# Four fused sequence layers on one core: the state matrices turned by VectorE and by way of memory, and the gate product in two passes over x

## The reference, cut to what matters

```python
x = x + y * mask                      # y: each head convolved with its kernel K[h], up to 1024 taps
x = x + x @ W1.T + 2 * sum_e gate[e] * (x @ A[e].T) @ B[e].T   # gate: softmax of the two best of 8 logits x @ Wr.T
x = x + x @ W2.T + 0.5 * (x @ lora_A[label]) @ lora_B.T        # label: one of 5, by batch row
x = x + x @ w_eff.T                   # w_eff: quantized weight plus a low-rank part
```

## Time and profile before

| | us |
|---|---|
| median of three runs | 1013.91 |
| lowest and highest of them | 1013.37, 1016.0 |
| the profiled execution | 1015.38 |
| its span, first to last instruction | 1013.5 |
| granted TensorE clock, mean over the span | 0.998 |

### The profile page before, as it was taken

The page is one execution under the profiler, slowest core; times in us unless marked ns, Lnnn a source line. Parts: engine busy times, 40 slices in busy tenths (PEclk is TensorE's granted clock), DMA queues, the critical chain, the costliest instruction groups (busy, mean ns, idle before and its releaser), DMA issues.

```text
span 1013.5 us, 16370 instructions
## 1 busy us (share of the span) xinstructions
PE 994.4 (98%) x4767; PEld 799.7 (79%) x4767; DVE 823.2 (81%) x1617; ACT 454.1 (45%) x867; POOL 285.6 (28%) x343
## 2 busy tenths in 40 slices
PE   6999999999999999999999999999999999999997
PEld 3455558888888878888888888888888888888886
DVE  5499897989855688888888888888888888888863
ACT  1352523552367354534544355443544445454431
POOL 6300100644444422232222322233222332223200
PEclk9999999999999999999999999999999999999999
DMA  8602010100202444454445545455454544545321
GB/s 293 123 22 77 7 42 1 42 1 1 42 1 46 73 81 86 84 104 82 85 80 92 101 77 90 76 104 93 74 91 77 104 89 78 88 81 104 64 41 42
DMA packets 314676, 74.44 MB, mean 73 GB/s; under 512 B 290434, under 2 KB 307138, under 8 KB 314642
## 3 DMA queue, kind: packets, MB, share of 16 engines
q1 hardware_dynamic: 313634, 73.28, 37.6%
q10 hardware_dynamic: 1008, 0.76, 0.3%
HBM read 57.08 MB, written 16.91 MB: 73 GB/s over the span
## 4 chain that ended last, share of the span: by engine, by line
PE 95%; ACT 2%; DVE 1%; issue 1%; ACTq 1%; DMA 0%; SPq 0%; DVEq 0%
PE bank L719 34%; PE bank L942 13%; PE bank L884 11%; PE bank L709 10%; PE bank L740 4%; PE bank L689 4%; PE bank L700 4%; PE bank L678 4%; PE bank L895 2%; PE bank L864 2%; PE bank L746 1%; PE bank L730 1%; PE bank L824 1%; PE bank L903 1%; PE bank L667 1%
## 5 line engine op out<-in xcount | busy, mean ns | idle before, releaser
L719 PE MATMUL bank<-Mh,strips_r 128*128 128x512 f32 x1020 | 289.1, 395 | 0.0
L719 PEld LDWEIGHTS bank<-Mh,strips_r 128*128 128x128 f32 x1020 | 189.8, 188 | 41.1
L1015 ACT ACTIVATE SK<-ZZ 64x448 f32<-64x448 f32 x128 | 73.8, 577 | 214.9 <-DVE ZZ L1352 212.6
L719 PE MATMUL bank<-Ml,strips_r 128*128 128x512 f32 x510 | 160.0, 395 | 0.0
L501 POOL TENSOR_TENSOR Cl<-QC,Ch 128x256 fp32r<-128x256 f32 x32 | 24.1, 755 | 445.5 <-ACT Ch L997 445.5
L1352 DVE SCALAR_TENSOR_TENSOR ZZ<-ZZ,coef 128x192 f32<-128x192 f32 (+1 forms) x256 | 116.5, 495 | 10.1 <-DVE ZZ L1343 0.3
L719 PEld LDWEIGHTS bank<-Ml,strips_r 128*128 128x128 f32 x510 | 95.9, 188 | 22.5
L884 PE MATMUL bank<-E,A 128*128 128x512 f32 (+1 forms) x352 | 112.1, 477 | 0.8 <-ACT A L1085 0.8
L709 PE MATMUL bank<-Mh,strips_r 128*128 128x296 f32 x512 | 110.8, 300 | 0.3 <-DVE strips_r L1371 0.3
L884 PEld LDWEIGHTS bank<-E,A 128*128 128x128 f32 x352 | 56.8, 191 | 51.6 <-issue 50.2
L709 PEld LDWEIGHTS bank<-Mh,strips_r 128*128 128x128 f32 x512 | 85.0, 188 | 6.9 <-DVE strips_r L1371 6.3
(11 more groups left out here) (303 smaller groups left out, 1794.5 us busy)
## 6 DMA issues: line engine op xcount, KB each, us to landing
X<-in_x SPq DMA_DIRECT2D x256, 64.0 KB, 2.8
XT<-in_x SPq DMA_DIRECT2D x256, 64.0 KB, 2.6
out_x<-O SPq DMA_DIRECT2D x62, 256.0 KB, 3.2
toep<-kpad SPq DMA_DIRECT2D x128, 64.0 KB, 2.2
E<-in_L_cond_W SPq DMA_DIRECT2D x8, 512.0 KB, 9.2
vq<-in_L_cond_weight SPq DMA_DIRECT2D x8, 512.0 KB, 3.6
W2s<-in_L_cond_W SPq DMA_DIRECT2D x7, 512.0 KB, 4.5
LA<-in_L_cond_lora_A SPq DMA_DIRECT2D x8, 80.0 KB, 3.6
```

What stands on the lines that cost most here:

```text
L719: pe.matmul(psO[nh][:, :], xs[:, c, :], ms[:, c, nh * BANK:(nh + 1) * BANK], start=(c == 0 and n == 0), stop=False)
L1015: act.activation(SK[ri * N:(ri + 1) * N, hh, :].rearrange("p (c b) -> p c b", b=B), ZZ[hh * N:(hh + 1) * N, :, ri, :], ACT.Copy).then_inc( ...
```

## The change

`state_transpose` stays for tiles 0, 1 and 2. From tile 3 on, VectorE turns QB in 32 x 32 blocks into a new buffer TB (`b_turn`), SyncE stores TB to memory and loads it back with the blocks in their places into a new buffer Bt (`swap_b`), ScalarE takes Bh from Bt (`bt_hi`), and VectorE takes Bl from Bt and Bh (`bt_lo`). `b_turn(i+3)` stands behind `s_lo` in tile i; `swap_b(i+3)` stands between the XT loads and the toep loads in tile i; `bt_hi(i+2)` and `bt_lo(i+2)` stand in tile i behind `c_hi` and behind the second `carry_across`. The first head's `chunk_states` waits for `z_out` itself, as the second's did. `low_in` runs 16 matmuls with the high half of x, after a wait for `x0h_done`, and then 8 with the low half, after the wait for `x0l_done`. On VectorE `low_lo` goes ahead of both `x0_lo`.

```diff
+    turned = nc.dram_tensor("turned", [P, HB * P], F32, kind="Internal").ap()
+    TB = place("TB", [P, HB, PARTS, SPAN], F32, at=at_turns + 4 * HB * 2 * P)
+    Bt = place("Bt", [P, HB, P], F32)
@@ sync
+                def swap_b(i):
+                    n = i - BY_PE
+                    sp.wait_ge(tb_done, n + 1)
+                    if n:
+                        sp.wait_ge(bt_loaded, 16 * PARTS * n)
+                    sp.dma_start(turned[:, :], TB[:, :, :, :].rearrange("p h k j -> p (h k j)")).then_inc(tb_stored, 16)
+                    sp.wait_ge(tb_stored, 16 * (n + 1))
+                    sp.wait_ge(bl_done, i)
+                    for k in range(PARTS):
+                        src = bass.AP(turned.tensor, k * SPAN, [[HB * P, SPAN], [P, HB], [SPAN * HB * P, PARTS], [1, SPAN]])
+                        sp.dma_start(Bt[k * SPAN:(k + 1) * SPAN, :, :].rearrange("p h (a j) -> p h a j", a=PARTS), src).then_inc(bt_loaded, 16)
...
                     if i + 3 < TILES:
+                        swap_b(i + 3)
                         load_within(i + 3)
@@ tensor
-                    if hh == 1 and not first:
+                    if not first:
                         pe.wait_ge(z_out, 2 * HB * i)
...
                 def low_in(i):
+                    pe.wait_ge(x0h_done, HB * i + HB)
+                    for c in range(NC):
+                        for n, ms in enumerate((Mh, Ml)):
+                            pe.matmul(psL[:, 0:LOWC], x0h[:, c, :], ms[:, c, L:MW], start=(c == 0 and n == 0), stop=False,
+                                      skip_group_check=True)
                     pe.wait_ge(x0l_done, HB * i + HB)
                     for c in range(NC):
-                        for n, (xs, ms) in enumerate(((x0h, Mh), (x0h, Ml), (x0l, Mh))):
-                            last = pe.matmul(psL[:, 0:LOWC], xs[:, c, :], ms[:, c, L:MW], start=(c == 0 and n == 0), stop=False,
-                                             skip_group_check=True)
+                        last = pe.matmul(psL[:, 0:LOWC], x0l[:, c, :], Mh[:, c, L:MW], start=False, stop=False, skip_group_check=True)
                     last.then_inc(lr_done, 1)
...
                     low_transpose(i)
-                    if next3:
-                        state_transpose(i + 3)
@@ scalar
+                def bt_hi(i):
+                    act.wait_ge(bt_loaded, 16 * PARTS * (i - BY_PE + 1))
+                    act.wait_ge(z_done, HB * i)
+                    act.activation(Bh[:, :, :], Bt[:, :, :], ACT.Copy).then_inc(bh_done, 1)
...
                         c_hi(i + 1)
+                    if next2 and not first:
+                        bt_hi(i + 2)
...
                         x0_hi(i + 1, 1)
-                    if next3:
-                        b_hi(i + 3)
@@ vector
+                def b_turn(i):
+                    dve.wait_ge(qb_step, Q_STEPS * (i + 1))
+                    hold(dve, "dve")
+                    dve.transpose(TB[:, :, :, :].rearrange("p h k j -> p (h k) j"),
+                                  QB[:, :, :, :].rearrange("p h k r -> p (h k) r")).then_inc(tb_done, 1)
+                    dve.wait_ge(tb_done, i - BY_PE + 1)
+                    dve.sem_inc(bT_done, 1)
+                def bt_lo(i):
+                    dve.wait_ge(bh_done, i + 1)
+                    dve.tensor_tensor(Bl[:, :, :], Bt[:, :, :], Bh[:, :, :].bitcast(F32), ALU.subtract).then_inc(bl_done, 1)
...
-                    if next2:
-                        b_lo(i + 2)
+                    if first:
+                        b_lo(2)
...
                         carry_across(i + 1, 1)
+                    if next2 and not first:
+                        bt_lo(i + 2)
...
                         s_lo(i + 1)
+                    if next3:
+                        b_turn(i + 3)
                     gated_lo(i)
...
                         select(i + 1, 1)
-                        x0_lo(i + 1, 0)
                     low_lo(i)
                     if next1:
+                        x0_lo(i + 1, 0)
                         x0_lo(i + 1, 1)
```

More of the change, by code:

```diff
@@ L165, in resid_stack_kernel @@
     toep = place("toep", [P, HB, 2, P], F32R, at=at_turns)
+    TB = place("TB", [P, HB, PARTS, SPAN], F32, at=at_turns + 4 * HB * 2 * P)
+    Bt = place("Bt", [P, HB, P], F32)
+    assert cursor[0] <= at_expo
     Vt = place("Vt", [P, H, SPAN], F32, at=region_q - 4 * NC * QO)
@@ L324, in resid_stack_kernel @@
         end_taken = sem("end_taken")
+        tb_done, tb_stored, bt_loaded = sem("tb_done"), sem("tb_stored"), sem("bt_loaded")
+        BY_PE = 3
         X_LOADS = HB * P // SPAN
@@ L747, in low_out, with tile @@
                     last.then_inc(out_full, 1)
-                def tile(i, next1, next2, next3, first=False):
+                def tile(i, next1, next2, first=False):
                     low_in(i)
@@ L968, in _ @@
                 pe.wait_ge(m_lo, len(mno))
-                tile(0, True, True, True, first=True)
-                with pe.Fori(1, LAST - 2) as i:
-                    tile(i, True, True, True)
-                tile(LAST - 2, True, True, False)
-                tile(LAST - 1, True, False, False)
+                tile(0, True, True, first=True)
+                with pe.Fori(1, LAST - 1) as i:
+                    tile(i, True, True)
+                tile(LAST - 1, True, False)
                 last_tile(LAST)
@@ L1048, in take_out, with tile @@
                         act.activation(O[:, nh * BANK:(nh + 1) * BANK], psO[nh][:, :], ACT.Copy).then_inc(out_taken, 1)
-                def tile(i, next1, next2, next3, first=False, second=False):
+                def tile(i, next1, next2, first=False, second=False):
                     if not first:
@@ L1059, in tile @@
                         c_hi(i + 1)
+                    if next2 and not first:
+                        bt_hi(i + 2)
+                    if next1:
                         states_out(i + 1, (0,))
@@ L1280, in _ @@
                 act.sem_inc(out_taken, 1)
-                tile(0, True, True, True, first=True)
-                tile(1, True, True, True, second=True)
-                with act.Fori(2, LAST - 2) as i:
-                    tile(i, True, True, True)
-                tile(LAST - 2, True, True, False)
-                tile(LAST - 1, True, False, False)
-                tile(LAST, False, False, False)
+                tile(0, True, True, first=True)
+                tile(1, True, True, second=True)
+                with act.Fori(2, LAST - 1) as i:
+                    tile(i, True, True)
+                tile(LAST - 1, True, False)
+                tile(LAST, False, False)
                 act.wait_ge(out_full, LAST + 1)
@@ L1425, in low_lo, with tile @@
                     dve.tensor_tensor(part, psT[RL:2 * RL, P:2 * P], part.bitcast(F32), ALU.subtract).then_inc(lowTl_done, 1)
-                def tile(i, next1, next2):
+                def tile(i, next1, next2, next3, first=False):
                     if next2:
@@ L1768, in _ @@
                     x0_lo(0, hh)
-                with dve.Fori(0, LAST - 1) as i:
-                    tile(i, True, True)
-                tile(LAST - 1, True, False)
-                tile(LAST, False, False)
+                tile(0, True, True, True, first=True)
+                with dve.Fori(1, LAST - 2) as i:
+                    tile(i, True, True, True)
+                tile(LAST - 2, True, True, False)
+                tile(LAST - 1, True, False, False)
+                tile(LAST, False, False, False)
 _INS = ["x", "itok_B_8_3872", "itok_B_0_7", "itok_B_0_2", "condB_codebook", "L0_cond_log_dt", "L0_cond_C",
```

## The result

| | before | after |
|---|---|---|
| median of 6 runs each | 1014.39 us | 1008.21 us |
| lowest and highest | 1013.37, 1016.0 | 1006.89, 1008.51 |
| span of the profiled execution | 1013.5 | 1006.5 |

The ratio is 0.9935, 95% interval 0.9925 to 0.9945. The changed kernel is faster by 6.2 us where 8.0 were forecast. Ratios are to the kernel before in the same series of runs.

A forecast was written before the change was run, and what follows sets the result against it. TensorE was taken as the bound. 29 tiles times 0.24 us (7.0), tile 29's 0.25 and tile 30's 0.7 make 8.0 us off the median 1013.91: 1005.9 us, range 1003 to 1012.

The forecast's parts named there:

- The bound: TensorE, 95% of the chain and busy through all of each 20.95 us tile; only shortening its stream or stalls pays.
- the halves need each other: At the tile seam: removing transposes alone brings nothing, mending the wait alone 0.03 us a tile, both together 0.24.
- The rival that all of the 0.20 of the earlier trace counts: All weight-load idle at the seam is a cost: 0.41 us a tile, 1001 us; chance 0.07.
- What it puts on VectorE: VectorE from seam to `s_lo`: 0.26 us lost, scan end unchanged, slack before `from_states` falling from 0.87 to 0.37.
- the 0.26 of the seam: At the seam both `x0_lo` end 0.26 us later than before, because `low_lo` goes first and waits for `low_hi`.
- the first rival: VectorE becomes the bound, `bt_lo` contending with GpSimd: half the gain lost, 0.12 us a tile left, 1009.5 us; chance 0.16.
- Tiles 29 and 30: Last two tiles: 0.25 us gained in tile 29, 0.7 in tile 30 from a shorter `low_lo` wait plus the seam.
- `b_turn` in the gap ahead of `gated_lo`: On VectorE, `b_turn` takes 0.37 us plus 0.2 of wait in a gap shrinking from 1.48 to 0.98: free.
- ScalarE's cover: Slack of `gated_hi` on ScalarE falls from 0.62 to about 0.12 us, the tightest; any excess reaches `gated_lo` and `low_gated`.
- The memory trip: TB's store and loads: `bt_hi` through by 577.9, VectorE at `bt_lo` about 579.3, so hidden with 1.4 us of cover.
- the late-trip rival: Store and load landings reaching 6.9 us make VectorE wait at `bt_lo` every tile; slow end 1031 us; chance 0.08.
- The sum: Whole kernel: 7.0 us from tiles 0 to 28, 0.25 from tile 29, 0.7 from tile 30; 8.0 us in all.

The follow-up runs named there:

- first kernel: Changed kernel with transposes on VectorE and the memory trip, but the old order of `low_in` and of the seam: 1014.12 us, ratio 0.9999 to the kernel before.
- second kernel: Kernel before the change, transposes still on TensorE, with only `low_in` in two passes and `low_lo` first: 1012.56 us, ratio 0.9984 to the kernel before.
- fifth kernel: Changed kernel with GpSimd's three QB operations moved behind `b_turn`, those on QC starting with the scan: 1005.27 us, ratio 0.9918 to the kernel before.
- kernel with two stores: Changed kernel with the store of TB to memory made twice in a row, each waited for, ahead of the loads: 1008.43 us, ratio 0.9943.
- kernel with three stores: Changed kernel with the store of TB to memory made three times in a row, each waited for, ahead of the loads: 1044.87 us, ratio 1.0302.
- four stores: Changed kernel with the store of TB to memory made four times in a row, each waited for, ahead of the loads: 1066.83 us, ratio 1.0523.
- the one with the exponential: Changed kernel with GpSimd's QB operations behind `b_turn`, plus one throwaway Exp on ScalarE ahead of tile 0: 1005.48 us, ratio 0.9909.
- last kernel: Changed kernel with GpSimd's QB operations behind `b_turn`, throwaway Exp ahead of tile 0, and first `x0_lo` step before `low_lo`: 1005.23 us, ratio 0.9905.
- fourth kernel: Changed kernel with all six of GpSimd's operations on QB and QC moved behind `b_turn`: 1008.57 us, ratio 0.9948 to the kernel before.

## Why the prediction was right, and by how much not

1. **The bound, and that the halves need each other: right.** TensorE's stream had no gap but the seam. The transposes alone gave 0.00 a tile (first kernel, 20.952), the seam alone 0.02 (second kernel, 20.930; forecast 0.03), both 0.23 where VectorE is not late: the fifth kernel's 20.719 stands against 20.71 forecast. The rival that all of the 0.20 of the earlier trace rows counts is out: no kernel had a mean tile under 20.71.

2. **What it puts on VectorE: the term that was mis-sized.** I let the end of the scan stay where it was, with ends of 0.3 us better and 0.4 worse, and kept 0.37 of the 0.87 us of slack. (The two don't fit together: I wrote that the 0.26 of the seam were included in that 0, and then the slack would have been 0.87 - 0.24 = 0.63. The 0.37 takes them off once more.) `bt_lo` cost the upper end: 0.85 instead of 0.42 us. I had laid out the sequence with GpSimd's operations excluding VectorE's, and let the first `x_lo` come ahead of them. It did (0.69 us); but `bt_lo` came behind one of 0.61 us, and the second `x_lo` with 1.22 behind the next. `s_lo` ended 0.26 later than forecast (0.11 of slack instead of 0.37), and `from_states` took 1.26 instead of 1.22 us. 0.04 x 28 = 1.1 us of the 1.0 to 1.8 that were missing. This is the first rival's mechanism, at a third of the size that I gave it (0.12). The Trainium skill, GPSIMD Engine Reference, section Key points, states that contention. The runs agree and give its size, 0.41 against 0.85 us. It is not a slowdown in proportion but the wait for a whole operation: in the kernel with two stores `bt_lo` of tile 11 began 0.19 us later and yet ended at the same point.

3. **Tiles 29 and 30: right.** 0.22 and 0.72, forecast 0.25 and 0.7; the wait for `low_lo` in tile 30 is 0.68 instead of 1.12.

4. **`b_turn` in the gap ahead of `gated_lo`: right that it is free.** The forecast left 0.98 - 0.57 = 0.41 us of the gap, and the row of L1452 above shows 0.41 of idle time. Both terms were off: the gap is 588.37 - 587.60 = 0.77, since `s_lo` ends later, and `b_turn`, 0.44 long (0.37 forecast), starts a little ahead of `s_lo`'s end and takes only 0.36 of it (587.96 - 587.60), where 0.57 was put in. ScalarE's cover, the tightest by the prediction with 0.12 us, is used up. `gated_hi` (L1066) follows the states' copies with no idle time ahead of it, where it had 0.62:

```profile
585.82 2.22 ACT L1036 ACTIVATE ZZ<-bank 64x448 f32<-64x448 f32 x4
588.06 0.28 ACT L1066 ACTIVATE hgTh<-bank 128x128 fp32r<-128x128 f32 x1
```

It costs nothing so far: `low_gated` takes 0.30 for its three matmuls in the chain, as before, and no wait for it shows.

5. **The memory trip: right.** `bt_hi` was to be through 3.6 us after `low_in`'s new start and `bt_lo` to start 5.0 after it; in tile 11 it is 3.69 and 4.97. The pieces differ: a load's issue takes 0.65 (2.58 / 4) and not 0.53, its landing 2.2 and not 2.7. The 4.97 is luck in part. The first `x_lo` took 0.69 instead of the 1.23 that I put in, and from its end to `bt_lo` it is 1.17 us (577.00 - 575.83, the latter being 575.14 + 0.69) where I had 0.65 for the two scan steps. The DMA share rose by 0.06 and not by 0.03. The kernel with three stores shows the late-trip rival at work: landings of 5.8 (607.87 - 602.06, three stores) + 2.2 = 8.0 us gave a tile of 22.05, where the rival's rule, 20.71 for 6.9 us and one for one from there, gives 21.8. With two stores it is 6.5 and nothing is lost. So the rival's threshold was right to some tenths. Its chance of 0.08 was for landings that never came near it: the store's slowest took 2.9 us, the loads' slowest 2.6. With four stores the rule gives 20.71 + 9.7 - 6.9 = 23.5, and the tile was 22.8: that far out it is no longer one for one. The store in the changed kernel, by its own view:

```profile
L395 SPq DMA_DIRECT2D turned<-TB x29: 340/432/497, 359.5 to 941.9; - x29
DMA to landing us min/median/max: 2.1/2.5/2.9
```

6. **The sum.** 8.0 us forecast, 7.0 by the spans and 6.2 by the medians. By the spans: 28 tiles gave 5.5 instead of 6.7, 1.2 short; tile 0 gave 0.1 instead of 0.24; tiles 29 and 30 0.94 instead of 0.95. That tile 0 began 0.65 earlier was in no forecast, although it is the seam's own wait: without this unforeseen gain the miss would have been larger.

The 0.8 us between spans and medians comes from ahead of tile 0, and the traces show from where. In some executions TensorE's granted clock is at its lower level, 1.2 GHz, for a stretch between 318 and 325 us. Over these 7 us the mean clock is 0.76 in the profiled executions of the kernel before, of the changed kernel and of the one with the exponential, 0.51 or 0.52 in the first, the second and the last kernel, and 1.00 in the other seven. Tile 0 begins at 340.6 us or later in the six with such a stretch and at 339.6 or earlier in the seven without. Set against the execution of a kernel that is the same up to there, the short stretch costs 0.8 to 1.2 us and the long one 2.4 to 2.6. The rest of the spread, some 1.2 us, arises in the first 30 us of the span and stays the same up to 313.

The profiled executions of before and after both have the short stretch, so their difference, 7.0, compares like with like. The medians don't. Of the six executions of the changed kernel two have a mean clock of 1.0 and took 1006.89 and 1007.17 us, four have 0.997 or 0.998 and took 1008.20 to 1008.51, and the median falls among the four. The six of the kernel before have no clock on record, but they fall in two groups as well, 1013.37 to 1013.91 and 1014.88 to 1016.0, three each, and the median lies between them. Group against group the gain is 6.5 and 7.7 us.

What stays open: why the clock falls in some executions and not in others. TensorE was busy for all of the 20 us from 290 to 310 and for 7.9 of the 8 us behind them both in the changed kernel, where the clock then fell, and in the fifth, where it did not. No experiment aimed at it.

## What to carry to other kernels

Where the one full engine also waits somewhere, taking work off it and mending the wait are one change: each alone can measure as nothing, and a stretch of the trace where one of them is already in force (a last tile that has nothing to prepare) says so in advance. Work moved from a bank to SBUF on VectorE can double in length beside GpSimd (0.42 to 0.85 us here); lay out both engines' operations on one clock as whole blocks that exclude one another, and then look where GpSimd's can go, checking the place that it moves to as closely as the one it leaves. A trip through memory of some 7 us from issue to use is free as long as its consumer has other work: find the last moment at which it is wanted, and measure it by making the trip longer. Where executions differ by a stretch at a low clock outside the part that was changed, compare those of like clock before a difference of medians is read.

## What the runs showed of the hardware

- VectorE against GpSimd, each operation as a whole: a subtraction of 128 x 256 with two inputs in SBUF 0.41 us alone and 0.85 behind a GpSimd operation; of 128 x 512, 0.68 and 1.22; an operation of GpSimd of 128 x 256 0.61 and, beside VectorE's, 1.10. A plain copy of 128 x 64 from SBUF to SBUF, with one input only, was 0.20 and 0.32: the one that undid the gain of the fourth kernel.
- A second store of the same 128 KB to the same place in memory takes 1.7 us where the first takes 2.5, and so do a third and a fourth (issues 1.7 to 1.8 us apart).
- One more stream of transfers, 0.06 of the DMA engines' time in a tile, left the others as they were: the median landings are 2.8 and 2.7 us for X before and after, 2.6 and 2.6 for XT, 2.2 and 2.3 for toep.
- The load of ScalarE's table for the exponential takes 1.28 us; moved ahead of the tiles it took 1.31 off tile 0. It is the only table load in any tile: the copies of all later tiles run with that table loaded.
- A stretch of TensorE at its lower clock level, 3.4 us long by its mean (0.76 over 7 us), made what follows 0.8 to 1.2 us later; one twice as long made it 2.4 to 2.6 later.
